# Attention's ramp in another order with its weighted sums on VectorE, and its residual taken by VectorE from PSUM

## The reference

```python
Wh1 = h @ W[:IN_C]
Wh2 = h @ W[IN_C:]
s1 = Wh1 @ a_w
s2 = Wh2 @ a_w
e = s1[:, None] + s2[None, :] + a_b
e = jnp.where(e >= 0, e, ALPHA * e)
e = jnp.where(adj > 0, e, NEG_BIG)
att = jax.nn.softmax(e, axis=1)
return att @ (h @ fc_w + fc_b)
...
x = x + _L0_gnn_ref(_layernorm(x, axis=-1), adj, L0_gnn_W, L0_gnn_a_w, L0_gnn_a_b, L0_gnn_fc_w, L0_gnn_fc_b)
```

## Time and profile before

| what | us |
|---|---|
| median of 3 runs | 1150.05 (1149.79 to 1150.12) |
| profiled execution | 1157.18 |
| its span | 1155.4 |
| TensorE, VectorE, ScalarE, GpSimd busy | 1024.5, 757.2, 618.9, 447.0 |
| products of attention (line 554) busy | 234.3 |
| score sum (line 420), 26 times | 114.6 |
| mask and maximum (line 426), 26 times | 100.0 |
| GpSimd's residual (line 266), 26 times | 90.0 |

### The profile page before, as it was taken

How to read it: one execution, slowest core, us unless ns; L and a number is a source line. 1 busy time by engine, 2 the same in 40 slices (tenths; PEclk the granted TensorE clock), 3 DMA queues, 4 the chain that set the end, 5 groups by cost and what they waited for, 6 DMA issues and landing times. The chain is left out here.

```text
span 1155.4 us, 23510 instructions
## 1 busy us (share of the span) xinstructions
PE 1024.5 (89%) x7616; PEld 823.4 (71%) x7617; DVE 757.2 (66%) x1598; ACT 618.9 (54%) x948; POOL 447.0 (39%) x363
## 2 busy tenths in 40 slices
PE   6649999999999689798987999999289999999992
PEld 5539989898989579687754887888156666666661
...
GB/s 382 193 295 269 222 253 223 256 218 254 225 85 1 113 74 38 90 76 20 1 119 70 174 242 217 226 228 256 248 38 51 51 54 55 55 53 49 53 47 23
DMA packets 72590, 161.51 MB, mean 140 GB/s; under 512 B 7505, under 2 KB 58449, under 8 KB 66513
## 3 DMA queue, kind: packets, MB, share of 16 engines
...
...
## 5 line engine op out<-in xcount | busy, mean ns | idle before, releaser
L554 PE MATMUL PS<-G,PT 128*128 128x256 f16 x2028 | 234.3, 273 | 0.0
L554 PEld LDWEIGHTS PS<-G,PT 128*128 128x128 f16 x2028 | 198.8, 98 | 22.5
L1576 PE MATMUL PS<-W,X 128*128 x708 | 164.0, 382 | 4.4 <-DVE X L1732 4.4
L1748 DVE SCALAR_TENSOR_TENSOR own_H<-PS,w_unscale,own_H 128x1024 f32<-128x1024 f32 x59 | 75.7, 1284 | 100.9 <-PE PS L1576 100.9
L1500 PE MATMUL PS<-own_H,adj_room 128*128 128x257 f16 x572 | 132.1, 277 | 0.0
L1502 PE MATMUL PS<-own_H,adj_room 128*128 128x256 f16 x572 | 132.1, 276 | 0.0
L1576 PEld LDWEIGHTS PS<-W,X 128*128 128x128 f16 x708 | 69.5, 98 | 84.0 <-issue 7.2
L420 DVE SCALAR_TENSOR_TENSOR score<-S2low,S1low,S2row 128x3327 f32<-128x3327 f32 x26 | 114.6, 4407 | 1.4 <-ACT S2low L299 1.4
L538 PE MATMUL PS<-ident,probs 128*128 128x128 f32 x676 | 91.7, 283 | 24.4 <-ACT probs L327 16.8
L1596 PE MATMUL PS<-adj_room,X 128*128 x472 | 111.6, 380 | 0.2 <-issue 0.2
L1816 POOL TENSOR_TENSOR X<-X 128x256 f32<-128x256 f32 x59 | 44.3, 750 | 159.6 <-ACT X L1461 157.2
...
## 6 DMA issues: line engine op xcount, KB each, us to landing
...
```

What stands on the lines that cost most here:

```text
L554: mm = nc.tensor.matmul(acc[u][:, 0:D], left, right, start=(j == 0 and n == 0), stop=(j == T - 1 and n == 2))
L1576: mm = nc.tensor.matmul(psHE[u][:, n * F1:(n + 1) * F1], left[u][:, k, :], W1[:, e, k, part, n * F1:(n + 1) * F1], start=(m == 0), stop=(m ...
L1748: v.scalar_tensor_tensor(hb[u][:, :], psHE[u][:, :], t["w_unscale"][:, :], b1[:, e, :], ALU.mult, ALU.add).then_inc(hb_ready, 1)
```

## The change

1. **Weighted sums.** u = W a is made by VectorE: W is loaded in its own layout, aw is loaded as a full row in every partition, and four multiply-and-sum instructions (`uw`) take the place of the matmuls. The means of fcw and of u are taken separately (`psM` from fcw, `psU` from uw), and centring writes `fcwx` straight from fcw. fcw moves to the head of the sync queue; aw comes first on ScalarE's queue, then W.
2. **Order of the ramp.** VectorE does the sums first, the statistics of group 0 after them, and those of group 1 before `gains(0)`. Later groups get `gains(n + 1)` and `row_moments(n + 2)` after the first pair of group n. ScalarE takes the root of the next group first, copies score chunks one or two tiles earlier, and makes the mask of tile 0 at the start of the last group. The score sum and the masking of tile 0 are split at column 2560; the first part stands before the last four `G_lo`.
3. **Residual.** `weigh` on ScalarE and `residual` on GpSimd are gone. VectorE does acc x rscale + X in one instruction, with acc read from PSUM, after the masking of the iteration and before the first `lo`. TensorE's products wait for it where they waited for `weigh`.
4. **A wait.** VectorE waits for the four bias additions (`fcb_added`) before it enters the row loop.

The store of zeros is the same in both.

```diff
...
         xT = PT[:, :, :].rearrange("p q n -> p (q n)").bitcast(F32).rearrange("p (t k n) -> p t k n", t=T, k=KD)
-        WT = score[1][:, 0:KD * 2 * D].rearrange("p (k n) -> p k n", k=KD)
-        fcw = score[1][:, KD * 2 * D:KD * 3 * D].rearrange("p (k n) -> p k n", k=KD)
+        W = score[1][:, 0:2 * KD * D].rearrange("p (k n) -> p k n", k=2 * KD)
+        fcw = score[1][:, 2 * KD * D:3 * KD * D].rearrange("p (k n) -> p k n", k=KD)
+        aw = score[1][:, 3 * KD * D:3 * KD * D + D]
+        uj = [score[1][:, (3 * KD + 1 + m) * D:(3 * KD + 2 + m) * D] for m in range(2 * KD)]
         raw = sb("raw", [P, 8 * P])
...
         unit = raw[:, 8 * P - P:8 * P]
-        aw = sb("aw", [P, KD])
+        uw, u_mean = sb("uw", [P, 2 * KD]), sb("u_mean", [P, 2])
         ab, ab_low = sb("ab", [P, 1]), sb("ab_low", [P, 1])
...
         S1low = sb("S1low", [P, T])
-        big, spent = sb("big", [P, 1]), sb("spent", [P, 1])
+        big, spent, part_max = sb("big", [P, 1]), sb("spent", [P, 1]), sb("part_max", [P, 2])
         small = lambda n: [sb(f"{n}{u}", [P, 1]) for u in range(2)]
         rowmax, shift_by, total, rtotal, rscale = (small(n) for n in ("rowmax", "shift_by", "total", "rtotal", "rscale"))
-        attended = [sb(f"attended{u}", [P, D]) for u in range(2)]
         blank = sb("blank", [P, ROW])
...
         x_stats, var_done, std_done, gained = sem("a_xstats"), sem("a_var"), sem("a_std"), sem("a_gain")
-        u_done, u_copied, mean_done, centred = sem("a_u"), sem("a_ucp"), sem("a_mean"), sem("a_centred")
+        u_done, u_summed, mean_done, centred = sem("a_u"), sem("a_usum"), sem("a_mean"), sem("a_centred")
+        u_added, parts_done, leaky_part_done = sem("a_uadd"), sem("a_parts"), sem("a_leaky_parts")
         row_done, row_copied = sem("a_row"), sem("a_rowcp")
...
         def _(sp):
+            sp.dma_start(fcw[:, :, :], dram["fcw"].rearrange("(k p) n -> p k n", p=P)).then_inc(fcw_in, 16)
             for n, (a, b) in enumerate(XG):
...
-            def residual(t, u):
-                if isinstance(t, int) and t == 0:
-                    pool.wait_ge(fcb_added, 16 * len(XG))
-                settled(pool, add_waits, (weighed, t + 1))
-                nc.gpsimd.tensor_tensor(X[:, t, :], X[:, t, :], attended[u][:, :], ALU.add).then_inc(x_ready, 1)
-
             def iteration(t, u):
...
                     split(t, u, 2)
-                if live(t - 2):
-                    residual(t - 2, u)
...
         def _(act):
-            act.dma_start(WT[:, :, :], dram["WT"].rearrange("(k p) n -> p k n", p=P)).then_inc(u_in, 16)
-            act.dma_start(aw[:, :], dram["aw"]).then_inc(u_in, 16)
-            act.dma_start(fcw[:, :, :], dram["fcw"].rearrange("(k p) n -> p k n", p=P)).then_inc(fcw_in, 16)
+            act.dma_start(aw, dram["aw"]).then_inc(u_in, 16)
+            act.dma_start(W[:, :, :], dram["W"].rearrange("(k p) n -> p k n", p=P)).then_inc(u_in, 16)
             act.dma_start(ident[:, :], dram["ident"]).then_inc(ident_in, 16)
...
-            def weigh(t, u):
-                settled(act, exp_waits, (acc_ready, t + 1), (scale_ready, t + 1), (x_ready, t - 1))
-                nc.scalar.activation(attended[u][:, :], acc[u][:, 0:D], ACT.Copy,
-                                     scale=rscale[u][:, :]).then_inc(weighed, 1)
-
             def iteration(t, u):
...
                     exponent(t + 1, 1 - u)
-                if live(t - 2):
-                    weigh(t - 2, u)
                 if live(t):
...
-            deviation(0)
             act.wait_ge(fcw_in, 16)
...
                                  accum_out=fsq[:, :]).then_inc(f_squared, 1)
+            deviation(0)
             act.wait_ge(f_summed, 1)
...
             act.wait_ge(ab_in, 16)
-            act.wait_ge(pad_set, 4)
+            act.wait_ge(pad_set, 5)
             for n, (a, b) in enumerate(XG):
-                if n > 0:
-                    deviation(n)
-                if n == len(XG) - 1:
+                if n + 1 < len(XG):
+                    deviation(n + 1)
+                else:
                     nc.scalar.activation(spent[:, :], big[:, :], ACT.Exp, scale=-1.0).then_inc(exp_waits, 1)
+                    no_edge(0, 0)
                 for i in range(a, b):
                     G_hi(i)
-                    if i % 4 == 3 and i >= 7:
-                        row_back((i - 7) // 4)
-            for c in range((T - 8) // 4 + 1, len(CK)):
-                row_back(c)
-            no_edge(0, 0)
+                    if i % 4 == 1 and i >= 5:
+                        row_back((i - 5) // 4)
+            row_back(len(CK) - 1)
             no_edge(1, 1)
...
+            def leaky_part(n, a, b):
+                dve.wait_ge(s_low, 1)
+                dve.wait_ge(row_copied, 2 * -(-b // (4 * P)))
+                v.scalar_tensor_tensor(score[0][:, a:b], S2low[:, a:b], S1low[:, 0:1], S2row[:, a:b], ALU.add,
+                                       ALU.max).then_inc(leaky_part_done, 1)
+
+            def masked_part(n, a, b):
+                dve.wait_ge(mask_ready, 1)
+                dve.wait_ge(leaky_part_done, n + 1)
+                v.tensor_tensor_reduce(score[0][:, a:b], score[0][:, a:b], bias[0][:, a:b], 1.0, -2 * FAR,
+                                       ALU.subtract, ALU.max, part_max[:, n:n + 1]).then_inc(parts_done, 1)
+
             def masked(t, u):
...
-                settled(dve, mask_waits, (mask_ready, t + 1), (leaky_ready, t + 1), (shift_ready, t - 1))
+                settled(dve, mask_waits, (mask_ready, t + 1), (leaky_ready, t), (shift_ready, t - 1))
                 v.tensor_tensor_reduce(score[u][:, 0:N], score[u][:, 0:N], bias[u][:, 0:N], 1.0, -2 * FAR,
...
                 dve.wait_ge(inverted, t + 1)
-                wait(dve, weighed, t - 1)
+                wait(dve, x_ready, t - 1)
                 v.tensor_scalar(rscale[u][:, :], rtotal[u][:, :], g_back[:, :], None, ALU.mult).then_inc(scale_ready, 1)
+
+            def residual(t, u):
+                dve.wait_ge(acc_ready, t + 1)
+                dve.wait_ge(scale_ready, t + 1)
+                v.scalar_tensor_tensor(X[:, t, :], acc[u][:, 0:D], rscale[u][:, :], X[:, t, :], ALU.mult,
+                                       ALU.add).then_inc(x_ready, 1)
...
                     masked(t + 2, u)
+                if live(t - 2):
+                    residual(t - 2, u)
                 if live(t):
...
+            dve.wait_ge(u_in, 32)
+            for m in range(2 * KD):
+                v.tensor_tensor_reduce(uj[m], W[:, m, :], aw, 1.0, 0.0, ALU.mult, ALU.add, uw[:, m:m + 1]).then_inc(u_done, 1)
+            dve.wait_ge(fcw_in, 16)
+            dve.wait_ge(mean_done, 1)
+            for k in range(KD):
+                v.scalar_tensor_tensor(fcwx[:, k, 0:D], psM[:, 0:D], -1.0 / D, fcw[:, k, :], ALU.mult,
+                                       ALU.add).then_inc(centred, 1)
+            dve.wait_ge(u_summed, 1)
+            v.tensor_scalar(u_mean[:, :], psU[:, 0:2], -1.0 / D, None, ALU.mult).then_inc(u_added, 1)
+            dve.wait_ge(u_added, 1)
+            for k in range(KD):
+                v.tensor_tensor(fcwx[:, k, D:D + 2], uw[:, k:k + 3:2], u_mean[:, :], ALU.add).then_inc(centred, 1)
             row_moments(0)
-            dve.wait_ge(fcw_in, 16)
-            for k in range(KD):
-                v.tensor_copy(fcwx[:, k, 0:D], fcw[:, k, :]).then_inc(u_copied, 1)
-            dve.wait_ge(u_done, 1)
-            for k in range(KD):
-                v.tensor_copy(fcwx[:, k, D:D + 2], psU[:, k:k + 3:2]).then_inc(u_copied, 1)
             dve.wait_ge(f_rooted, 1)
...
             v.tensor_scalar(g_scale[:, :], frecip[:, :], FULL / ROW_BOUND, None, ALU.mult).then_inc(f_chain, 1)
-            dve.wait_ge(mean_done, 1)
-            for k in range(KD):
-                v.scalar_tensor_tensor(fcwx[:, k, :], psM[:, 0:D + 2], -1.0 / D, fcwx[:, k, :], ALU.mult,
-                                       ALU.add).then_inc(centred, 1)
             dve.wait_ge(ab_in, 16)
...
             dve.wait_ge(f_chain, 4)
+            row_moments(1)
+            gains(0)
+            early = CK[-2][0] * P
             for n, (a, b) in enumerate(XG):
-                if n > 0:
-                    row_moments(n)
-                gains(n)
                 row_scores(a // 2)
...
                         row_scores(q + 1)
+                    if 2 * q + 4 == T:
+                        leaky_part(0, 0, early)
+                        masked_part(0, 0, early)
                     G_lo(2 * q)
                     G_lo(2 * q + 1)
+                    if 2 * q == a:
+                        if n == 0:
+                            dve.wait_ge(s_ready, 2)
+                            v.tensor_scalar(S1low[:, 0:4], S12[:, 0:4, 0], ALPHA - 1.0, None, ALU.mult).then_inc(s_low, 1)
+                        if n + 1 < len(XG):
+                            gains(n + 1)
+                        if n + 2 < len(XG):
+                            row_moments(n + 2)
```

(37 more changed lines are left out.)

## The result

Both kernels were timed on one chip: after 1145.15 us (median of 6, 1142.62 to 1147.11), before 1149.95 (median of 6), ratio 0.9958 with the interval [0.9948, 0.9969]. That is 4.8 us faster, where 1145.1 was predicted. The profiled execution of after took 1146.19, span 1144.4.

What follows compares the result with a forecast made beforehand. In the loop, a two-iteration chain through VectorE, with its GpSimd lock, was taken to set the pace, just above TensorE's floor. Ramp -2.0, loop -2.3, tail -0.65 and wait 0 gave -4.95 off 1150.05: 1145.1 us, range 1139.5 to 1150.5.

Steps and rivals of the forecast that it cites:

- Loop (-2.3): Row loop: two iterations fall from 23.2 to 22.95 us, 2.3 us in all, between -4.8 and 0.
- The scaling's 0.36: Row loop: removing ScalarE's scaling brings everything behind it on the two-iteration chain 0.36 us earlier.
- the 0.27: Row loop: without GpSimd's addition, VectorE's masking drops from 3.89 to 3.62 us, 0.27 off the two-iteration chain.
- The lock: Row loop: GpSimd and VectorE operations stand for each other; whether the new residual does too, no row showed with certainty.
- the price of 0.38: Row loop: VectorE's new residual adds 0.38 us per tile to the chain, estimated from the pitch of similar operations.
- Tail (-0.65): Last row of attention: 0.76 us replaces 1.41, so the next stage starts 0.65 us earlier.
- Ramp (-2.0): Before the row loop: first row maximum and start of rows 2.0 us earlier, between -5 and +0.5.
- The new wait (0): Entry to row loop: bias additions end at 68 to 69, VectorE arrives at 72.5, so it costs 0.
- a wait of VectorE on them: Masking of tile 2: VectorE standing for the bias additions would make the forecast wrong; 3 us to spare was expected.
- the 714 packets: Software DMA queue: bias additions taken as having done 714 of 3328 packets at 42 us, as before the change.
- that cover shrinks by as much as the ramp is faster: Entry to row loop: the 3 us between the additions' end and VectorE's arrival shrink one for one with ramp gain.
- the bias additions come last: Rival at row loop entry: additions end at 77.7, tile 2's masking starts 3.2 later, total 1150.3 us; chance 0.13.

Runs made afterwards that it cites:

- the idle addition: The changed kernel plus a GpSimd operation adding zeros to zeros in the old addition's place, its output never read; ratio to before 0.997, period 11.552.
- the second trace of after: The changed kernel run once more without any edit, in another group on another chip; ratio to before 0.9958, period 11.480.
- the faster ramp: The changed kernel with later statistics spread over tile pairs and tile 0's mask behind tile 23's high half, wait left early; ratio to before 0.9955.

## Why the prediction was right, and where not

**Loop (-2.3): right, with its mechanism.** -2.29 in the trace, period 11.488 in the range 11.47 to 11.50. The scaling's 0.36 was measured by itself (0.36 to 0.38). The residual took 0.40 where 0.38 was taken, and the run with the residual after the low half shows that this slot is on the chain, and that TensorE's floor lies right below (22.71 for two, 22.74 by the earlier trace rows). For GpSimd's addition the 0.27 fits the sum (-0.36 - 0.27 + 0.40 = -0.23; measured 2 x -0.109 = -0.22), but the idle addition gave 0.13, so this term is supported only by its sign and the sum. With the residual alone the sum itself came out at 2 x -0.075 = -0.15.

**The lock: not taken by the residual.** That the price of 0.38 has no standing for GpSimd in it was the author's estimate; the traces bear it out. In the kernel with the residual after the low half it starts at 214.20 while GpSimd's cast runs (213.82 to 214.86), and lasts 0.48. Of that trace's 26 residuals 22 overlap this cast, and all 26 last 0.47 or 0.48. In after 22 of 26 have GpSimd's shift (L254, 0.19) beside them, and all 26 last 0.48, the last one of attention with nothing of GpSimd beside it among them. The gain of the loop says the same: with the shift's 0.19 on the chain as well, the sum for two iterations would be -0.36 - 0.27 + 0.40 + 0.19 = -0.04, and -0.22 was measured.

```profile
213.82 1.04 POOL L260 CAST PT<-raw 128x1024 f16<-128x1024 f32 x1 [0.29 <-ACT raw L308]
```

```profile
214.20 0.48 DVE L445 SCALAR_TENSOR_TENSOR X<-PS,rscale,X 128x256 f32 x1
```

**Tail (-0.65): -0.80.** A little under. From the start of ScalarE's last scaling (381.63) to the end of the statistics (383.47) it was 1.84 before; from the start of the residual (377.82) to their end (378.96) it is 1.14. These 0.70 are close to the forecast; the other 0.1 lies between TensorE's last product and that start.

**Ramp (-2.0): the direction right, the size not settled, the reasons in part.** The first projection came at 14.09 (13.9), the waits of TensorE were 2.02, 0.36 and 3.17 (2.7, 0.5, 3.5), two pairs ran at half rate (one or two), the first maximum at 61.79 (60.1 to 62.1). But W at 11 was one draw: in twelve traces it came between 8.37 and 10.99, and in the second trace of after the first maximum was at 58.93, outside of the forecast. In the two traces of after the start of the rows gained 1.42 and 0.61. The old ramp moves as well: with the residual alone its masking of tile 2 came 0.67 earlier than before. So the gain lies between 0.4 and 1.4 at that masking, under the -2.0. In the second trace the ramp had gained 4.3 by the first maximum, and the wait took 3.3 of it back.

**The new wait (0): this step failed.** The additions were to end at 68 to 69 with VectorE coming at 72.5; a wait of VectorE on them was named as a sign of being wrong. In the first trace of after they ended at 70.1 and VectorE, coming at 72.9, waited for nothing. In the second they ended at 73.3 and it stood 3.48; in three of the variants it stood 1.47 to 4.88 (6.54 with the faster ramp).

Two terms of the walk were wrong. The first is the backlog. The prediction carried over the 714 packets that the additions had done at 42 us in before. In after they had done 411, and 443 in the second trace: the two first stores of zeros were issued at 31.90, not 30.28, and the other queue moved 1097 packets in 36 to 42 us, not 618. The rows are 38 to 42 us of the first trace; before 38 the additions had moved nothing.

```profile
q0 software_dynamic: 411, 0.42, 65.3%
q1 hardware_dynamic: 511, 0.52, 50.3%
```

At the prediction's own 112 to 194 packets per us, the 303 missing ones are 1.6 to 2.7 us, an estimate from these rows: they alone move the end to about 70 to 72. The second term is "that cover shrinks by as much as the ramp is faster". It shrinks from both sides. With an earlier ramp the mask of tile 0 is made earlier, so adjacency tile 2 is asked for at 44.13 (46.74 in the first trace) and tile 3 at 54.92 (57.79), and each load, with the store behind it, takes its turns from the software queue (111 packets in 1 us beside the other queue's 112, 194 without it). The end of the additions is drawn out, too: the rows are the queue's packets in 66 to 70 us of the first trace of after, then in 70 to 72 of the second.

```profile
q0 software_dynamic: 10, 0.01, 1.3%
q1 hardware_dynamic: 469, 1.58, 98.2%
```

```profile
q0 software_dynamic: 26, 0.02, 6.2%
```

Ten packets are spread over four microseconds while the other queue moves 469; why is not shown. The rival "the bias additions come last" was right as a mechanism and too dear as a price. Its 77.7 does not come out of its own terms either: 42 + 14.1 + 18.3 leaves 182 of the 2614 packets, which gives 76 to 77.

**The total.** By the first trace it is -1.4 - 2.3 - 0.8 = -4.5, by the second -3.9 (its last statistics start 0.65 later), where -4.95 was forecast. The ramp's lower gain and the wait stayed within the ramp's range. That the median hit 1145.1 to the tenth is luck: the interval of the ratio alone is 2.4 us wide, and one execution differs from the next by more behind attention (764.1 to 775.0 over the traces).

**The span.** That the sum was taken off the median, not off the profiled 1157.18, was needed: that execution is 7 us over the median, and it spends 6.7 more than the profiled one of after in the aggregation.
